# Last layer of a four-layer convolution stack as 1x1 products and tiled depthwise taps, plane loads three strips ahead, edge copies behind layer 0's first loads, and one box part moved

## The reference, cut to what matters

```python
h = einsum('bchw,oc->bohw', x, w_in)              # 48 -> 192 channels
h = conv(h, w_dw, 3x3, 'SAME', one filter per channel)
x1, x2 = split(h, 2, axis=1)                      # 96 each
h = gelu(x1) * x2
y = einsum('bchw,oc->bohw', h, w_out)             # 96 -> 48 channels
f = rfft2(8x8 patches of y) * fft_w;  y = irfft2(f)
```

## Time and profile before

| | us |
|---|---|
| median of 3 runs (lowest, highest) | 20823.17 (20798.16, 20833.35) |
| the profiled execution, its own time | 20805.98 |
| its span from first to last instruction | 20804.4 |
| PE busy | 18912.8 (91%) |
| DVE busy | 13400.9 (64%) |
| POOL busy | 10324.5 (50%) |
| ACT busy | 7497.1 (36%) |

### The profile page before, as it was taken

The page is one execution under the profiler, slowest core; times in us unless marked ns, Lnnn a source line. Parts: engine busy times, 40 slices in busy tenths (PEclk is TensorE's granted clock), DMA queues, the critical chain, the costliest instruction groups (busy, mean ns, idle before and its releaser), DMA issues. The chain is left out here.

```text
span 20804.4 us, 500656 instructions
## 1 busy us (share of the span) xinstructions
PE 18912.8 (91%) x172464; PEld 11734.2 (56%) x172464; DVE 13400.9 (64%) x22319; ACT 7497.1 (36%) x22720; POOL 10324.5 (50%) x8692
## 2 busy tenths in 40 slices
PE   6998998989999989899999898999997889898999
PEld 4665555466655554566555546665555456565666
DVE  4444445666667776666677766666777677777744
ACT  4664332155542221555422215553322122222222
POOL 0000000077767740777677407776773088787800
PEclk9999999999999999999999999999999999999999
DMA  3331112655544446555344465553444666666633
GB/s 94 72 72 44 36 37 92 135 114 116 114 102 113 114 126 137 116 120 119 100 113 112 129 134 118 119 120 101 113 116 128 136 145 147 151 150 148 151 87 77
DMA packets 932864, 2323.52 MB, mean 112 GB/s; under 512 B 276340, under 2 KB 528504, under 8 KB 844124
## 3 DMA queue, kind: packets, MB, share of 16 engines
q1 hardware_dynamic: 500560, 1364.68, 28.1%
q0 software_dynamic: 430080, 928.96, 16.9%
HBM read 1915.53 MB, written 385.13 MB: 111 GB/s over the span
## 5 line engine op out<-in xcount | busy, mean ns | idle before, releaser
L1842 POOL DMA_INDIRECT e_got<-table,e_idx x6144 | 7483.8, 1218 | 2376.3 <-issue 1624.3
L1858 POOL DMA_INDIRECT e_got<-table,e_idx x2048 | 2539.9, 1240 | 690.1 <-issue 537.0
L1012 PE MATMUL b_p_conv<-b_z,b_diag 32*32 32x512 f32 x76032 | 2810.7, 599 | 0.0
L531 PE MATMUL a_p_qk<-a_wst,a_stack 125*128 125x192 f32 x12288 | 2463.9, 337 | 273.0 <-ACT a_qh L662 212.3
L531 PEld LDWEIGHTS a_p_qk<-a_wst,a_stack 125*128 125x128 f32 x12288 | 2023.2, 191 | 709.0 <-issue 438.6
L1114 ACT ACTIVATE b_z<-b_p_z 128x256 f32<-128x256 f32 x2112 | 845.0, 400 | 3875.9 <-PE b_p_z L976 3522.7
L1896 DVE TENSOR_TENSOR e_got<-e_got,e_wt 128x1536 f32<-128x1536 f32 x1024 | 1779.0, 1753 | 698.5 <-DMA e_got<-table,e_idx 646.3
L976 PEld LDWEIGHTS b_p_z<-const,b_ym 128*128 128x128 f32 x8448 | 1149.8, 196 | 1199.0 <-issue 696.9
L1201 DVE TENSOR_TENSOR b_ym<-b_p_in,b_mask 128x512 f32<-128x512 f32 x1056 | 729.9, 691 | 1653.1 <-PE b_p_in L968 1652.9
L976 PE MATMUL b_p_z<-const,b_ym 128*128 128x128 f32 x8448 | 1524.7, 304 | 100.2 <-ACT b_z L1114 94.0
L2142 PE MATMUL d_p_v<-d_xs,d_ws 125*128 125x512 f32 x4608 | 1379.7, 447 | 59.7 <-issue 56.2
(11 more groups left out here) (291 smaller groups left out, 35717.4 us busy)
## 6 DMA issues: line engine op xcount, KB each, us to landing
e_got<-table,e_idx POOLq DMA_INDIRECT x8192
b_x<-planes SPq DMA_DIRECT2D x264, 395.1 KB
a_stack<-in_xp SPq DMA_DIRECT2D x256, 387.0 KB
c_stack<-planes SPq DMA_DIRECT2D x256, 387.0 KB
d_stack<-planes SPq DMA_DIRECT2D x512, 193.5 KB
table<-i_acc SPq DMA_DIRECT2D x256, 384.0 KB, 2.3
b_xr<-planes SPq DMA_DIRECT2D x264, 197.5 KB
planes<-b_out SPq DMA_DIRECT2D x264, 197.5 KB
```

Source lines behind the costliest of these rows:

```text
L531: m = pe.matmul(dst_, st[:, row, dx + 128 * t:dx + 128 * t + 128], wst[:, dx, 0:2 * C2], start=(dx == 0), stop=False)
L1012: mm = pe.matmul(p_conv[q // 2 * 2 + r % 2][BLK * c:BLK * (c + 1), :], diag[g][BLK * r:BLK * (r + 1), k, :], zs[BLK * r:BLK * (r + 1), g, ...
L1842: pool.indirect_dma_start(out=self.got[q][:, t, c * REC:(c + 1) * REC], out_offset=None, in_=self.flat, in_offset=bass.IndirectOffsetOnAxi ...
L1858: pool.indirect_dma_start(out=self.got[q][:, t, c * REC:(c + 1) * REC], out_offset=None, in_=self.flat, in_offset=bass.IndirectOffsetOnAxi ...
```

## The change

Layer 3: SP loads 49 planes of 9 rows twice, to partitions 0 and 64, in two DMAs a strip, asked for once the strip that used the buffer has been through the 1x1 product. PE makes the 1x1 product in fp32 (`hidden_big`, two matmuls at a time in two groups of rows; `hidden_small`, eight), ACT copies it to `z`, PE adds the nine taps as diagonal matmuls (`taps_big`: nine rounds of 16 for 128 outputs; `taps_small`: six rounds of eight for the other 64, which stand twice so that a matmul adds two taps), split into six pieces with the back half of the strip before between them. GELU and product work on 128 partitions, three times a strip instead of six. `upper` and `lower` are gone from layer 3, with the 16 weight loads (six now) and the split of weights.

Core of the diff:

```diff
-                    for k in range(2):
-                        for h in range(2):
-                            load_half(sp, src, b, k * SROWS, h, stack[k], rest[k], loaded[k][h])
+                def load(s, k):
+
+                    for r in (0, 64):
+                        sp.dma_start(x[k][r:r + CP, :, :], planes(src, b, 0, CP, s * SROWS + 2, NX)).then_inc(loaded[k], 16)
...
-                    if load:
-                        refill(s, k, 1)
+                    if more_x:
+
+                        sp.wait_ge(h_ready, (first + s + 2) * 4)
+                        sp.sem_inc(turn, 1)
+                        load(s + 3, 1 - k)
...
+                def hidden_big(i, xs, row):
+
+                    r = 64 * i
+                    return pe.matmul(p_z[:, i, :], w[r:r + CP, 0:128], xs[r:r + CP, row:row + QROWS, 1:1 + W], start=True, stop=True)
+
+                def hidden_small(bank, r, xs, row):
+
+                    for t in range(4):
+                        y = row + t % 2
+                        mm = pe.matmul(p_z[BLK * t:BLK * t + BLK, bank, :], w[r:r + CP, 128 + BLK * t:128 + BLK * t + BLK],
+                                       xs[r:r + CP, y:y + QROWS, 1:1 + W], start=True, stop=True)
+                    return mm
...
+                        for i in range(lo, hi):
+                            dy, dx = divmod(i, 3)
+                            for row in range(4):
+                                for c in range(4):
+                                    q = PERM[row][c]
+                                    mm = pe.matmul(p_v[q // 2 * 2 + row % 2][BLK * c:BLK * (c + 1), :], diag[0][BLK * row:BLK * (row + 1), i, :],
+                                                   z[k][BLK * row:BLK * (row + 1), 0, dy:dy + SROWS, dx + QX * q:dx + QX * (q + 1)],
+                                                   start=(i == 0), stop=(i == 8))
...
+                            for row in range(2):
+                                for c in range(4):
+                                    mm = pe.matmul(p_v[row][BLK * c:BLK * (c + 1), :], diag[1][64 * row:64 * (row + 1), i, :],
+                                                   z[k][64 * row:64 * (row + 1), 1, y:y + SROWS, dx + QX * c:dx + QX * (c + 1)],
+                                                   start=(i == 0), stop=(i == 5))
...
-                def take_lower(k, w, h):
-                    dve.wait_ge(upper_done, (w + 1) * 2)
-                    dve.wait_ge(conv_ready, (w - 1) * 3)
-                    lower(dve, xs[h][1][:], stack[k][:, HROWS * h:HROWS * (h + 1), :], xs[h][0][:], lower_done)
-                    lower(dve, xe[h][1][:], rest[k][:, HROWS * h:HROWS * (h + 1), 0:W], xe[h][0][:], lower_done)
```

Start and layer 0:

```diff
-                for t in (p1, p2):
-                    sp.dma_start(t[:, :, 0, :], xp[:, :, 0, :]).then_inc(edges, 16)
-                    sp.dma_start(t[:, :, H + 1:H + 10, :], xp[:, :, H + 1:H + 10, :]).then_inc(edges, 16)
-                    sp.dma_start(t[:, 0, 1:H + 1, :], xp[:, 0, 1:H + 1, :]).then_inc(edges, 16)
                 sp.wait_ge(const_loaded, 16)
-                sp.wait_ge(edges, 96)
...
-                    if boxes and front:
-                        for part in ((1, 2) if k % 2 else (0,)):
-                            boxes.part(dve, u, k // 4, k // 2 % 2, part)
+                    if boxes and front and back:
+                        box_parts(u, k)
...
+                        if boxes and not back:
+                            box_parts(u, k)
```

More of the change, by code:

```diff
@@ new lines, in hidden_small, with hidden @@
+                def hidden_small(bank, r, xs, row):
[4 more added lines that the diff above has]
+                    return mm
+                def hidden(n, xs, j):
+                    g, h = divmod(j, 2)
+                    pe.wait_ge(z_copied, n * 4 + j)
+                    pe.sem_inc(turn, 1)
+                    for i in range(2):
+                        row = 2 * QROWS * h + QROWS * i
+                        mm = hidden_small(i, 64 * i, xs, row) if g else hidden_big(i, xs, row)
+                    mm.then_inc(h_ready, 1)
@@ L2149, in conv_small @@
[L2149 to L2162 removed]
+                    pe.matmul(p_v[0][:, 0:NW], fold[:], win[:], start=True, stop=True).then_inc(folded, 1)
@@ L2164, in step @@
+                    pe.wait_ge(w_ready, 2 * (b + 1))
+                    hidden_big(0, x0, 0)
+                    hidden_small(1, 0, x0, 0).then_inc(folded, 1)
+                    pe.wait_ge(loaded0, (b * U + 1) * 32)
+                    pe.wait_ge(zrow_ready, n0 + 1)
+                    for j in range(4):
+                        hidden(n0, x[0], j)
                 def step(v, r, n, front, back, more):
                     m = n - 1
+                    k = r % 2
+                    units = turned(v, r) if boxes and back else []
@@ new lines, in taps_small @@
+                    def taps_small(lo, hi):
+                        if lo == 0:
+                            pe.wait_ge(g_ready, n * 3 + 1)
+                            pe.sem_inc(turn, 1)
+                        for i in range(lo, hi):
+                            y, dx = divmod(i, 3)
+                            for row in range(2):
[3 more added lines that the diff above has]
+                                                   start=(i == 0), stop=(i == 5))
+                                    if c == 0 and row < beats(9 + i):
+                                        boxes.beat(mm)
+                        if hi == 6:
+                            mm.then_inc(conv_ready, 1)
@@ new lines, in step @@
+                    turn_box(0)
+                    if front:
+                        taps_big(0, 3)
+                    if back:
+                        w_out(0)
+                    turn_box(1)
+                    ahead(1)
+                    if front:
+                        taps_big(3, 6)
+                    if back:
+                        spectrum(0)
+                    ahead(2)
+                    if front:
+                        taps_big(6, 9)
+                    if back:
+                        inverse(0, 0)
+                        w_out(1)
@@ new lines, in step @@
+                    if back:
+                        spectra(0)
+                    if more:
+                        copy_hidden(n + 1, z[1 - k], 1)
+                        copy_hidden(n + 1, z[1 - k], 2)
+                    if front:
+                        act.wait_ge(conv_ready, n * 2 + 1)
+                        act.wait_ge(g_ready, n * 3)
+                        for h in range(2):
+                            act.activation(ga[h][:], p_v[2 * h][:], ACT.Gelu).then_inc(gelu_ready, 1)
@@ L2340, in step @@
[L2340 to L2361 removed]
+                        dve.tensor_tensor(rows, p_c[0:CP, :].rearrange("p (t y x) -> p t y x", y=SROWS, x=16), rows, ALU.add).then_inc(res_ready, 1)
```

413 lines of the change are left out of this document (199 added, 214 removed).

## The result

The changed kernel takes 20741.63 us (median of six runs, 20734.71 to 20759.78) against 20820.78 (six runs, 20798.16 to 20837.4) on the same chip. The ratio is 0.9963, 95% interval 0.9953 to 0.9974: 79 us or 0.37% less, where 260 were forecast. The profiled execution took 20743.57 us, 62 less than that of before; the medians differ by 79.

A forecast was written before the change was run, and what follows sets the result against it. POOL issuing gathers was taken to bound the joint stage, PE the last image. From the profiled 20,806 us, -200 (`lower`), -13 (last image), -31 (edge copies) and -3 (box part) gave -247: 20,560 us, range 20,450 to 20,765.

The forecast's parts named there:

- PE in the joint stage 28.6, less than POOL's 30.7: Joint stage, us per strip: PE's need stays below POOL's new pace, so PE still waits.
- the changes between images, taken at nothing: Layer 3's image starts: fewer weight loads against four product-and-copy pairs in sequence; 0 us, bounds -20 and +20.
- edge copies: Kernel start: the first load no longer waits for the edges and goes out at about 7 us; -31 us.
- box part: Start of layer 0 with boxes: DVE makes the products first; 1 us for each of three images, -3 us.
- last image, with its start: Last image, where PE sets the pace: 0.4 us less for each of 32 strips, -13 us.
- `lower` stretches gathers: Joint stage: DVE's `lower` lengthens POOL's gathers beside it; removing it from layer 3 gives -200 us.
- The rest 8.4, which stays: PE in layer 3: the 8.4 us of a last-image strip outside the convolution stays as it was.
- B': Rival: PE at 31.6 us a strip, 32.2 in the joint stage; time 20,830 us; chance 0.13.
- case A: POOL still bounds the joint stage, with shorter gathers; 20,560 us, own range 20,490 to 20,630; chance 0.60.
- case C: Rival: `lower` doesn't stretch gathers, so the joint stage keeps its POOL rate; 20,760 us; chance 0.08.
- The mean falls to about 1140: Joint stage: POOL's mean gather goes from 1240 to about 1140 ns while the median stays.
- B: Rival: matmuls in two groups of 64 rows don't run side by side, strip 36.8 us; 21,500 us; chance 0.06.

The follow-up runs named there:

- a lighter PE: Changed kernel with four of layer 3's six `taps_small` rounds left out, but for two matmuls of 64 columns in each: 20603.25 us, 217 less than before.
- the first experiment: Kernel before, with layer 3's `lower` instructions replaced by copies of two columns of one row, matmuls as many as before: 20624.11 us, 188 less.

## Why the prediction was wrong

In short: the step that failed was "PE in the joint stage 28.6, less than POOL's 30.7". PE needs 30.7 in a steady strip and loses more at each jump, so that it took over part of the bound and ate a share of what the shorter gathers gave. Two smaller terms failed too: the changes between images, taken at nothing, and the mean gather, which fell less far.

The sum was -247; by the table and the traces it should have read:

| term | forecast | measured |
|---|---|---|
| edge copies | -31 | -29 |
| box part | -3 | -8 |
| joint stage, with the changes between its images | -200 | -68 |
| last image, with its start | -13 | +28 |
| sum | -247 | -77 |

The first two measured terms are means over several traces, the last two those of one pair of traces. That pair itself differs by 62 us, the medians by 79.

- **Edge copies and box part: right.** In the first six profiles layer 1 of image 0 begins at 1902 us on average with the old start (three kernels) and at 1873 with the new; at image 3 the difference is 37. The run with the old layer 3 has 36 for both together.
- **`lower` stretches gathers: right, in mechanism and size.** -188 by itself against -200. The working was less good than its result: I shared the excess by time, but by the fit a us of weighing costs more (0.81) than one of `lower` (0.51), and `lower` overlaps a gather for 182 ns on average, 373 of its 464 us: 0.51 x 373 = 190. With the 0.39 of the gathers that overlap `lower` alone it would be 145, so how the 188 are made up is less sure than that they are.
- **"PE in the joint stage 28.6, less than POOL's 30.7": this step failed.** PE needs 30.7 in a steady strip and 32.2 on the mean of a turn of six. Of the parts that I had priced, nine rounds of `taps_big` are 10.1 (10.3 forecast), six of `taps_small` 5.6 (5.4), the 1x1 products 2.1 and 1.9 (2.1 and 1.8): together 19.7 for 19.6. What I had not priced is what made it. "The rest 8.4, which stays" is 9.3: `w_out`, `spectrum` and `inverse` are as many instructions as before, but `inverse` is now 0.93 to 1.02 a piece (3.49 a strip before, 3.90 now), `w_out` 3.81 for 3.51 and `spectrum` 1.61 for 1.41. Each piece now stands between tap pieces of another shape, which is the likely reason; no run tested it. The gathers and the beats together add 0.8 (10.86 for the nine rounds, 10.06 in the last image). The transposes of boxes take 0.73 on the mean and wait 0.25 for the bank. And the jump, which the timeline of before showed and I never looked for: 3.7 us and more for six strips, which a PE that waits for POOL can hide and one that sets the pace can't.
- **What that cost.** 57 us of the joint stage: so much comes back with a lighter PE, and so much without jumps. So it is not the steady strip by itself (30.7 against POOL's (1.168 + 0.30) x 21.33 = 31.3), but strip and jumps together. POOL's account closes: 205 us off the 3192 between first and last gather would have been 2987, measured are 3113, and of the 126 the mean gather makes 57 and the time at a standstill 69 (98 for 29). Of those 69 a light PE or the loss of the jumps gives back 42 to 44. The rival that came nearest is B', which had PE at 32.2 in the joint stage; its time was wrong because the last image's strips are 29.05, not 31.6. That 20,742 lies inside the stated range at all is chance: case A's own range ends at 20,630, only the end put there for case C, 20,760, reaches so far, and C's mechanism is refuted by the first experiment.
- **"Between images: 0" failed too.** I had seen that four pairs of product and copy stand one behind another and priced them at 2 us each. They take 3.3 each, as the clock is at half; mask, fold and the head's products ahead of them take 9, the next strip's first product 2: 24.2 us from the end of the load wait to the first taps (17645.10 to 17669.30), where before 10.1 followed the end of the wait (the first convolution began at 17738.14). The wait is 6 us shorter, 13 for 19, so 8 us net in this change; POOL's idle time outside its 0.305 rose from 29 us to 54 or 56 with a light PE or without jumps, all of it where images change (60 of the changed kernel's 98).
- **"The mean falls to about 1140": it is 1168**, 28 x 2048 = 57 us more. With `lower` gone and the old layer 3 it is 1152; the other 11 to 21 ns came with the new layer in every kernel that has it. In the fit the weighings cost 0.81 us per us of overlap in the changed kernel and 0.74 in the one without `lower`. Why is left open; no run was aimed at it.
- **The last image** has 32 x (29.05 - 28.41) = 20 us from the strips and about 5 more from the jumps (13 us come back when they are written out, 8 in the kernel before).
- Handshakes and loads at nothing: right as far as can be seen. A lighter PE and the kernel without jumps end at the same joint stage, and no wait of the single banks shows as what bounds it. Case C is ruled out by the first experiment, B by 0.94 a round of `taps_small`.

## What to carry to other kernels

When a change takes the bound away from one engine, count the next engine's pace with all that its slack used to hide: jumps, starts, switches between shapes and the traffic of the others, and not with its best strip. Here two engines ended within a few per cent of each other (3092 us for PE without gathers, 3136 for POOL with a light PE), and together they took 3193, longer than either. A part of the schedule that "stays" is to be measured beside its new neighbours.

## What the runs showed of the chip

- A DVE instruction with two SBUF inputs costs a gather issued beside it some 0.4 to 0.8 us per us of overlap, by how it is counted. One with an input in PSUM costs nothing (947 ns beside it, 947 alone). A one-input copy in SBUF costs less but not nothing (1.29 us beside two copies of 0.69).
- A backward jump costs PE 2.3 us idle and a slow piece behind it (4.81 for 3.42 us) where instructions are as small as these, and some 26 us for seven jumps in layer 1. The forecast had nothing for it.
- Rounds of 32x32 matmuls take 5% longer while gathers run (3.52 for 3.36 us a piece), although they neither touch the gathers' buffers nor wait for them; the larger matmuls of the kernel before do not (2.46 us for nine in the joint stage and alone).
- The granted clock can fall again right behind a filling. With 8.4 us of matmuls on constants at an image's start it read 0.50 at their beginning, 0.95 at their end, and 0.50 from 4 us behind them on, for 20 us in which PE was busy for 18.5; the first strip then ran at 0.96.
